# Transposing the second graph layer's weight through two PSUM banks instead of four, one batch earlier on VectorE

## Chip, cores and metric

The kernel runs on one core of a Trainium2 chip. The metric is the device time of one execution in microseconds (us). Engines are named as in the profile: PE is TensorE (PEld its weight loads), DVE VectorE, ACT ScalarE, POOL GpSimd, SP the engine that issues most DMAs.

## What is computed

The input is x (1250 nodes x 512, f32) and a list of 40,000 edges `src`, `dst`, sorted by `dst`. Four layers are added to x one after the other, each on the layer norm of what it gets:

```python
x = x + _L0_gnn_ref(_layernorm(x), edge_index, L0_gnn_Ws, L0_gnn_Wb, L0_gnn_a_w, L0_gnn_a_b)   # 8-head graph attention
x = x + _L0_ffn_ref(_layernorm(x)[None], L0_ffn_Wg, L0_ffn_bg, L0_ffn_We, L0_ffn_be)[0]          # one expert of 16, for all nodes
x = x + _L1_gnn_ref(_layernorm(x), edge_index, L1_gnn_W, L1_gnn_b)                               # h = x @ W.T + b, normed sum over edges, relu
x = x + _L1_ffn_ref(_layernorm(x)[None], L1_ffn_Wr, ..., L1_ffn_b2)[0]                           # one expert of 8 per node
```

The change concerns `L1_gnn_W` (512 x 512), which the third layer multiplies by in transposed form. The transposing is done long before that layer, during the first one.

## The kernel before

Nodes lie in T = 10 tiles of 128, features in K = 4 blocks of 128. The engines run one instruction stream each, in the order written, and meet only at semaphores.

**The counting stage.** The edges are turned into a dense matrix C of counts (source x target). 184 pairs of an edge group and a window of 16 targets are handled in NB = 23 batches of LB = 8 pairs. All four loops below run over the same batches b = 0 to 22, each engine at its own place:

- DVE makes the one-hot matrices of a batch in two halves, `half_onehots(b, 0)` and `half_onehots(b, 1)`, each two instructions of line 916 (one for L_ring, one for R_ring) and each adding 4 to the semaphore `onehots`. The rings hold two batches, so a half waits (line 929) until the pairs of batch b - 2 that used the same half are counted.
- PE runs for each pair `count` (three matmuls, line 1382, waits for `onehots`) and `merge` (one matmul, line 1389, adds what C holds). The order on PE is merge of pair k, count of pair k + 1, then `between(b, k)`. After k = 5 it also loads the addresses of the next batch into registers (line 1457, the helper of line 290).
- ACT copies the counts of each pair back into C (line 531). Pair k of PE's merge waits for the copy of pair k - 1.

**Work that rides along** in the same loops, for b in BEGIN (one tile t = b - 1 for b = 1 to 10): layer norm statistics on DVE (line 815), the normed rows on ACT (517), their transpose on PE (1295), the copy and the rest in f16 (509, 838), then the linear layer of the attention on PE, `lin_a` (1341, 1342) in batch b + 2, and its evacuation on DVE, `evac_a` (858, 860) in batch b + 4, between the two halves. The last tile, t = 9, has its `lin_a` in batch 12 and its `evac_a` in DVE's batch 14, followed there by `scores()` (864 to 867), which gives the thresholds of the attention.

**The second graph layer's weight.** B_GW = 12. For k = 0 to 3:

- PE: `second_weights(k)` in batch 12 + k, after pair 6: four transposes (line 1354) into the bank `gw_bank(k)`, one of the PSUM banks 6, 2, 4, 3. It waits for the last or the last but one `evac_a` (line 1352), since `lin_a` used banks 2 to 5.
- ACT: at the end of batch 12 + k, `gWT[:, 0, k, :]`, the high f16 part (line 600), signals `weight_hi`.
- DVE: at the start of its batch 15 + k, before `half_onehots`, waits for `weight_hi` and takes the low f16 part from the same bank (line 949), signals `weight_lo`.

**The thresholds.** B_CS = 17. PE transposes them after pair 6 of that batch (`thresholds`, line 1362) into banks 3, 4 and 5, after all four `weight_lo`. ACT copies them out at the end of the batch (604), SP writes them to DRAM (338) and reads them back spread over the partitions (343).

After batch 22 ACT loads its Exp table and makes four exponentials (606 to 609), DVE the first head's values (988), and the attention's main stage begins (633, 1025, 1030 and the matmuls of 1486).

Of the kernel before, what the change touches and what calls it, by code (L numbers as in the profile page):

```python
# [16 lines left out]
T = (NODES + P - 1) // P  # L17
NP = T * P
LAST = NODES - (T - 1) * P
K = D // P  # L20
# [35 lines left out]
BEGIN = {1 + t: t for t in range(T)}  # L56
LIN_SLOTS = ((0,), (1, 2), (), (3, 4), (5, 6), (7,), (8, 9), (10, 11))
B_GW = max(BEGIN) + 2
B_CS = B_GW + K + 1
EPS = 1e-5  # L60
FILL_H = 24
SLOPE = 0.2
# [2 lines left out]
def gnn_ffn_kernel(nc, x_d, src_d, dst_d, Ws_d, Wb_d, aw_d, ab_d, Wg_d, bg_d, We_d, be_d, gW_d, gb_d,  # L65
                   Wr_d, br_d, W1_d, b1_d, W2_d, b2_d, out_d):
    ctx = ExitStack()
    with ctx:
# [5 lines left out]
        def sem(name):  # L74
            if name not in sems:
                sems[name] = ctx.enter_context(nc.semaphore(name))
            return sems[name]
# [189 lines left out]
        bank = [ctx.enter_context(nc.psum_tensor(f"bank{i}", [P, 512], F32)) for i in range(8)]  # L267
# [20 lines left out]
        def targets(engine, off):  # L288

            _, at = nc.values_load_multi_w_load_instructions(  # L290
                wk[0:1, bass.ds(off, LB)], engines=[engine], min_val=0, max_val=NP - WN,
                skip_runtime_bounds_check_because="the groups' windows come from targets in 0 to NP, clipped to the last window")
            return at
# [3 lines left out]
            return bank[(0, 1, 7)[(base + k) % 3]] if isinstance(base, int) else bank[k % 2]  # L297

        def gw_bank(k):
            return bank[(6, 2, 4, 3)[k]]  # L300

        def counts_at(at, k):

# [195 lines left out]
        def _(a):  # L499
# [73 lines left out]
            for b in range(NB):  # L573
# [23 lines left out]
                if b - B_GW in range(K):  # L597
                    k = b - B_GW
                    a.wait_ge(sem("gwT_psum"), k + 1)
                    act(gWT[:, 0, k, :], gw_bank(k)[:, :], ACT.Copy, scale=WS).then_inc(sem("weight_hi"), 1)  # L600
                if b == B_CS:
                    for i, n in enumerate((4, 4, 2)):
# [199 lines left out]
        def _(v):  # L802
# [9 lines left out]
            def ln_stats(n, xt, keep=None):  # L812
                i = n % 2
                m = mv[:, i, :] if keep is None else keep
                link(V.bn_stats(st[:, i, :], xt))  # L815
                link(V.bn_aggr(m, st[:, i, :]))
                V.tensor_scalar(ve[:, i:i + 1], m[:, 1:2], EPS, None, ALU.add).then_inc(sem("ln_var"), 1)  # L817
# [11 lines left out]
            def ln_scale(n):  # L829
                i = n % 2  # L830
                v.wait_ge(sem("ln_sd"), n + 1)
                link(V.reciprocal(rs[:, i:i + 1], sd[:, i:i + 1]))
                V.scalar_tensor_tensor(nm[:, i:i + 1], mv[:, i, 0:1], -1.0, rs[:, i:i + 1], ALU.mult, ALU.mult).then_inc(sem("ln_rs"), 1)  # L833

            def xT_low(n, b, xt16):

                v.wait_ge(sem("xT_hi"), n + 1)
                V.tensor_tensor(xt16[:, 1, :, :], b[:, :].rearrange("p (k m) -> p k m", k=K), xt16[:, 0, :, :],
                                ALU.subtract).then_inc(sem("xT_ready"), 1)
# [16 lines left out]
            def evac_a(t):  # L856
                v.wait_ge(sem("linA"), t + 1)
                V.scalar_tensor_tensor(Wx[:, t, :, 0:F], bank[2 + t % 2][:, :].rearrange("p (h f) -> p h f", h=H), 1.0 / WS, Wb_bc,
                                       ALU.mult, ALU.add)
                V.scalar_tensor_tensor(sc[:, t, :], bank[4 + t % 2][:, 0:2 * H], 1.0 / WS, cb, ALU.mult, ALU.add).then_inc(sem("evacA"), 1)  # L860

            def scores():
                v.wait_ge(sem("evacA"), T)
                link(V.tensor_tensor(atb, sc[:, :, 0:H], ab_bc.unsqueeze(1).to_broadcast([P, T, H]), ALU.add))
                V.tensor_scalar(thr, atb, -1.0, None, ALU.mult).then_inc(sem("thr_made"), 1)
                V.tensor_scalar(steep, sc[:, :, H:2 * H], STEEP, None, ALU.mult)
                V.tensor_reduce(asmax, sc[:, :, H:2 * H].rearrange("p t h -> p h t"), AX.X, ALU.max).then_inc(sem("asmax"), 1)
# [16 lines left out]
            def passes():  # L884
                link(V.tensor_scalar(kt[0:1, :], iotaK[0:1, 0:MAXPASS], float(NPAIR), None, ALU.mult))
                link(V.tensor_scalar(kt[0:1, :], kt[0:1, :], bank[4][0:1, NPAIR:NPAIR + 1], None, ALU.is_lt))
                link(V.tensor_reduce(grp[0:1, 6:7], kt[0:1, :], AX.X, ALU.add))
                V.tensor_copy(npass[0:1, :], grp[0:1, 6:7]).then_inc(sem("npass_ready"), 1)
# [36 lines left out]
            def half_onehots(b, half):  # L925
                n = LC // 2
                c = slice(half * n, (half + 1) * n)
                e = slice(b * LC + half * n, b * LC + (half + 1) * n)
                at_least(v, "counted", (b - 2) * LB + (half + 1) * (LB // 2))
                onehot(L_ring[:, b % 2, c, :], iota_lo, loT[:, e, :], n, P)  # L930
                onehot(R_ring[:, b % 2, c, :], iota_q, qT[:, e, :], n, RW).then_inc(sem("onehots"), LB // 2)

            def first_onehots():
                n = LC // 4
                for q in range(4):
                    c = slice(q * n, (q + 1) * n)
                    onehot(L_ring[:, 0, c, :], iota_lo, loT[:, c, :], n, P)
                    onehot(R_ring[:, 0, c, :], iota_q, qT[:, c, :], n, RW).then_inc(sem("onehots"), LB // 4)

            pair_tables(0)  # L940
            for b in range(NB):
                if b == 1:
                    v.wait_ge(sem("ld_x"), 64)
                if b in BEGIN:
                    ln_stats(BEGIN[b], x[:, BEGIN[b], :])
                if b - 3 - B_GW in range(K):
                    k = b - 3 - B_GW
                    v.wait_ge(sem("weight_hi"), 2 + k + 1)
                    V.scalar_tensor_tensor(gWT[:, 1, k, :], gw_bank(k)[:, :], WS, gWT[:, 0, k, :],
                                           ALU.mult, ALU.subtract).then_inc(sem("weight_lo"), 1)  # L950
                if b:
                    half_onehots(b, 0)
                    if b - 4 in BEGIN:
                        evac_a(BEGIN[b - 4])
                        if BEGIN[b - 4] == T - 1:
                            scores()
                    half_onehots(b, 1)
                else:
                    first_onehots()
                    passes()  # L960
                if b == 2:
                    v.wait_ge(sem("weight_hi"), 1)
                    V.scalar_tensor_tensor(W016[:, 1, :, :], W0.rearrange("p k h f -> p k (h f)"), WS, W016[:, 0, :, :],
                                           ALU.mult, ALU.subtract).then_inc(sem("weight_lo"), 1)
                if b == 3:
                    v.wait_ge(sem("weight_hi"), 2)
                    V.scalar_tensor_tensor(Wa[:, 1, :, :].rearrange("p k c -> p (k c)"), bank[5][:, 0:K * 2 * H], WS,
                                           Wa[:, 0, :, :].rearrange("p k c -> p (k c)"), ALU.mult, ALU.subtract).then_inc(sem("weight_lo"), 1)
                if b - 1 in BEGIN:
                    ln_scale(BEGIN[b - 1])  # L970
                if b - 2 in BEGIN:
                    t = BEGIN[b - 2]
                    xT_low(t, bank[6], xTs[:, t % 2, :, :, :])
# [316 lines left out]
        def _(pe):  # L1290
# [55 lines left out]
            def second_weights(k):  # L1346

                if k == 0:
                    pe.wait_ge(sem("xT_ready"), T)
                    pe.wait_ge(sem("ld_gw"), 16)  # L1350
                if k >= 1:
                    pe.wait_ge(sem("evacA"), T if k == K - 1 else T - 1)
                for o in range(K):
                    ins = nc.tensor.transpose(gw_bank(k)[:, o * P:(o + 1) * P], gW[:, o, k * P:(k + 1) * P], ident[:, :])
                ins.then_inc(sem("gwT_psum"), 1)

            def thresholds():
                pe.wait_ge(sem("thr_made"), 1)
                pe.wait_ge(sem("weight_lo"), 2 + K)
                for i, n in enumerate((4, 4, 2)):  # L1360
                    for q in range(n):
                        ins = nc.tensor.transpose(bank[3 + i][0:H, q * P:(q + 1) * P], thr[:, 4 * i + q, :], ident[:, :])
                    ins.then_inc(sem("thrT_psum"), 1)
# [49 lines left out]
            def between(b, k):  # L1413
# [12 lines left out]
                if k == LB - 2:  # L1426
                    if b - B_GW in range(K):
                        second_weights(b - B_GW)
                    if b == B_CS:
                        thresholds()  # L1430
# [281 lines left out]
```

## Time and profile before

| what | us |
|---|---|
| median of the 3 runs | 585.64 |
| lowest and highest of them | 584.92, 589.37 |
| the profiled execution | 585.64 |
| its span in the profile | 583.9 |
| part of it outside the span | 1.74 |
| mean granted clock of PE | 0.96 of full |

The span starts with the first instruction and ends with the last. A row of a timeline gives the start, the duration, the engine, line and operation, and in brackets how long the engine sat idle before it and who released it. DVE and ACT rows overlap their successor by some 0.08 to 0.1 us at their end, so times of a sequence are best taken from start to start. The chain of waits leads back from the last instruction, at each step to what released it.

### The profile page before, as it was taken

The numbers are of one execution on the slowest core, as the hardware profiler recorded it, in microseconds if no ns is written. First come the engines' busy times: TensorE is split into PE (matmuls) and PEld (weight loads), VectorE is DVE, ScalarE is ACT, GpSimd is POOL, SyncE is SP. The second block draws the span as 40 slices with busy tenths as digits, with TensorE's granted clock in tenths as the row PEclk, the third lists the DMA queues.
The fourth block names the chain that finished last, engine by engine and source line by source line (L and its number), as shares of the span: only waits on it lengthen the run. The fifth ranks groups of instructions, "written<-read, shape, count | busy, mean of one in ns | idle before, by whom it ended". The sixth has DMA issues, their size and how long they took to land.

```text
span 583.9 us, 11915 instructions
## 1 busy us (share of the span) xinstructions
PE 502.4 (86%) x4561; PEld 371.5 (64%) x4562; DVE 460.2 (79%) x907; ACT 331.2 (57%) x644; POOL 70.9 (12%) x83
## 2 busy tenths in 40 slices
PE   1869999987579999998999479996999967999995
PEld 1757777775468888887777334453566636767752
DVE  7989999898899999986898556875565645786781
ACT  5365555667879999985674423344222218665740
POOL 3000000000000000000000300213233320222242
PEclk9989999999699999999999689999999977999999
DMA  7960000011011111100000183000011149367111
GB/s 192 358 238 2 1 2 1 3 33 63 0 47 47 47 47 48 46 3 1 1 2 2 50 326 147 1 1 3 0 39 38 55 154 382 111 207 234 58 52 49
DMA packets 25305, 45.12 MB, mean 77 GB/s; under 512 B 6961, under 2 KB 7205, under 8 KB 25248
## 3 DMA queue, kind: packets, MB, share of 16 engines
q1 hardware_dynamic: 23264, 39.16, 19.7%
q0 software_dynamic: 1952, 5.18, 2.4%
q8 instruction: 38, 0.62, 0.5%
q14 instruction: 19, 0.16, 0.1%
q10 hardware_dynamic: 32, 0.01, 0.0%
HBM read 33.23 MB, written 11.95 MB: 77 GB/s over the span
## 4 chain that ended last, share of the span: by engine, by line
PE 47%; DVE 32%; issue 11%; ACT 4%; POOL 3%; DMA 1%; ACTq 1%; POOLq 0%; DVEq 0%
PE bank L1317 8%; PE bank L1654 7%; PE bank L1642 6%; DVE big L916 6%; PE bank L1341 4%; DVE work L1030 4%; PE bank L1382 4%; PE bank L1389 3%; PE bank L1499 2%; PE bank L1486 2%; PE bank L1564 2%; PE bank L1295 2%; DVE rings L1030 2%; POOL row L475 2%; DVE work L988 2%
## 5 line engine op out<-in xcount | busy, mean ns | idle before, releaser
L916 DVE TENSOR_TENSOR big<-mid 128x1536 f16<-128x1536 f16 (+1 forms) x96 | 91.6, 1011 | 0.0
L1486 PE MATMUL bank<-big,work 128*128 128x130 f16 x1080 | 67.8, 224 | 12.0 <-DVE work L1030 11.6
L1382 PE MATMUL bank<-big 128*128 128x160 f16 x552 | 72.2, 248 | 2.6 <-DVE big L916 2.6
L1486 PEld LDWEIGHTS bank<-big,work 128*128 128x128 f16 x1080 | 64.2, 100 | 14.6 <-DVE work L1030 7.5
L1382 PEld LDWEIGHTS bank<-big 128*128 128x128 f16 x552 | 52.0, 111 | 4.8 <-DVE big L916 4.2
L1564 PE MATMUL bank<-mid 128*128 128x512 f16 x200 | 45.9, 379 | 3.3 <-POOL mid L449 3.3
L633 ACT ACTIVATE mid<-aux,small 128x1280 f16<-128x1280 f32 x36 | 47.4, 1350 | 1.5 <-DVE work L1030 1.1
L1499 PE MATMUL bank<-big,mid 128*128 128x260 f16 x400 | 47.2, 275 | 0.1
L531 ACT ACTIVATE big<-bank 128x160 f32 x92 | 28.0, 304 | 27.4 <-PE bank L1389 25.9
L1499 PEld LDWEIGHTS bank<-big,mid 128*128 128x128 f16 x400 | 38.2, 96 | 7.5 <-issue 0.3
L531 ACT ACTIVATE mid<-bank 128x160 f32 x92 | 27.8, 302 | 25.4 <-PE bank L1389 24.2
L815 DVE BATCH_NORM_STATS2 st<-row 128x6 f32<-128x512 f32 x40 | 27.7, 692 | 17.9 <-POOL row L475 17.2
L504 ACT ACTIVATE sd<-ve 128x1 f32<-128x1 f32 x40 | 8.1, 201 | 57.2 <-DVE ve L817 57.2
L1341 PE MATMUL bank<-big,rings 128*128 128x512 f16 x120 | 38.6, 378 | 0.0
L459 POOL DMA_INDIRECT out<-aux x16 | 25.8, 1611 | 81.6 <-DVE aux L1232 79.2
L1389 PE MATMUL bank<-mid,ident 128*128 x92 | 28.1, 305 | 8.2 <-ACT big L531 4.0
L1295 PE MATMUL bank<-ident,rings 128*128 128x128 f32 x120 | 19.4, 285 | 17.8 <-ACT rings L517 15.3
L1486 PE MATMUL bank<-big,rings 128*128 128x130 f16 x520 | 32.0, 220 | 2.9 <-DVE rings L1030 1.9
L1564 PEld LDWEIGHTS bank<-mid 128*128 128x128 f16 x200 | 19.6, 101 | 23.5 <-issue 3.8
L1486 PEld LDWEIGHTS bank<-big,rings 128*128 128x128 f16 x520 | 29.9, 98 | 4.0 <-DVE rings L1030 2.4
L444 POOL TENSOR_TENSOR mid<-mid,ident 128x128 f16<-128x128 f16 x10 | 5.3, 564 | 212.4 <-PE bank L1499 212.4
L517 ACT ACTIVATE rings<-row,nm,rs 128x512 f32<-128x512 f32 x30 | 24.3, 810 | 10.6 <-DVE nm L833 10.6
(293 smaller groups left out, 1090.5 us busy)
## 6 DMA issues: line engine op xcount, KB each, us to landing
big<-in_L_ffn_W SPq DMA_DIRECT2D x10, 1024.0 KB, 9.0
mid<-in_L_ffn_W SPq DMA_DIRECT2D x6, 1024.0 KB, 13.6
xperm_scratch<-work SPq DMA_DIRECT2D x1, 5753.0 KB, 19.2
aux<-thr_scratch SPq DMA_DIRECT2D x8, 640.0 KB, 3.8
aux<-xperm_scratch SPq DMA_DIRECT2D x8, 523.0 KB, 3.7
row<-in_x SPq DMA_DIRECT2D x1, 2304.0 KB
aux<-in_L_gnn_Ws SPq DMA_DIRECT2D x4, 256.0 KB, 4.4
work<-in_L_gnn_W SPq DMA_DIRECT2D x1, 1024.0 KB, 14.4
```

What stands on the lines that cost most here:

```text
L531: ins = act(counts_at(at[k], k), count_bank(base, k)[:, 0:RW].rearrange("p (d s) -> p s d", s=T), ACT.Copy)
L633: act(zmask[i % NZ], thr_bc[:, h % 2, :], ACT.Sigmoid, bias=steep[:, s, h:h + 1], scale=-STEEP).then_inc(sem("z_made"), 1)
L916: return V.tensor_tensor(out.rearrange("p c (v two) -> p c v two", two=2), values.rearrange("p (v two) -> p v two", two=2).unsqueeze(1).to ...
L1030: V.tensor_tensor(weighted[i % NC], zmask[m % NZ], C[:, s, :], ALU.mult).then_inc(sem("cz_made"), 1)
L1317: ins = mm(out, xt16[:, xp, k, :], w16[:, wp, k, :], start=i == 0 and k == 0, stop=i == 2 and k == K - 1)
L1341: mm(bank[2 + t % 2][:, :], xt, W016[:, wp, k, :], start=j == 0, stop=last)
L1382: mm(count_bank(base, k)[:, 0:RW], L_ring[:, slot, k * CH + j, :], R_ring[:, slot, k * CH + j, :], start=j == 0, stop=False)
L1389: ins = mm(count_bank(base, k)[:, 0:RW].rearrange("p (d s) -> p s d", s=T), ident16[:, :], counts_at(at[k], k), start=False, stop=True)
L1486: ins = mm(acc_region(h, t), weighted[i % NC][:, t * P:(t + 1) * P], VP[:, s, part, h, :, :].rearrange("p b f -> p (b f)"), start=False, s ...
L1499: ins = mm(bank[2 * (t % 2) + g2][:, 0:4 * FE].rearrange("p (h f) -> p h f", f=FE), C[:, s, t * P:(t + 1) * P], VP[:, s, part, 4 * g2:4 * ...
L1564: ins = mm(bank[6 + t % 2][:, :], C[:, s, t * P:(t + 1) * P], hp[:, s, part, :], start=s == 0 and part == 0, stop=s == T - 1 and part == 1)
L1654: ins = mm(bank[4 + 2 * (e % 2) + j][0:m, :], hT16[:, e % 2, hp_, k, j * P:j * P + m], W16[e % 2][1][:, wp, k, :], start=False, stop=n == ...
```

## The change

Only two banks, 6 and 2, serve for the four transposed blocks. PE's `second_weights` for k = 2 and 3 waits until DVE has taken the low part of block k - 2 out of the bank. DVE takes the low part of block k at the start of batch 14 + k instead of 15 + k. The thresholds are transposed and copied in batch 16 instead of 17. ACT's copies of the high part stay where they are.

```diff
-B_CS = B_GW + K + 1
+B_CS = B_GW + K
...
         def gw_bank(k):
-            return bank[(6, 2, 4, 3)[k]]
+            return bank[(6, 2)[k % 2]]
...
-                if b - 3 - B_GW in range(K):
-                    k = b - 3 - B_GW
+                if b - 2 - B_GW in range(K):
+                    k = b - 2 - B_GW
                     v.wait_ge(sem("weight_hi"), 2 + k + 1)
                     V.scalar_tensor_tensor(gWT[:, 1, k, :], gw_bank(k)[:, :], WS, gWT[:, 0, k, :],
                                            ALU.mult, ALU.subtract).then_inc(sem("weight_lo"), 1)
...
-                if k >= 1:
-                    pe.wait_ge(sem("evacA"), T if k == K - 1 else T - 1)
+                if k == 1:
+                    pe.wait_ge(sem("evacA"), T - 1)
+                if k >= 2:
+                    pe.wait_ge(sem("weight_lo"), 2 + k - 1)
```

## Rows read from the trace of the kernel before

**Rows 1.** The page: the span, and the costliest group of instructions.

```profile
span 583.9 us, 11915 instructions
...
L916 DVE TENSOR_TENSOR big<-mid 128x1536 f16<-128x1536 f16 (+1 forms) x96 | 91.6, 1011 | 0.0
```

**Rows 2.** Busy time by stretch: stretch, length, engines (instructions), PEclk, DMA share, GB/s.

```profile
80.00:105.50 25.50, 25.18 (x246) 18.82 (x243) 22.93 (x35) 13.39 (x41) 0.00 (x0) 1.00 0.01 2
105.50:123.00 17.50, 15.43 (x161) 13.01 (x158) 17.38 (x24) 11.91 (x40) 0.99 (x1) 1.00 0.01 1
123.00:142.50 19.50, 16.42 (x167) 13.25 (x165) 19.50 (x22) 13.09 (x43) 0.00 (x0) 1.00 0.22 71
```

**Rows 3.** The chain of waits, 105 to 143 us: start, us, what.

```profile
105.55 0.69 DVE mid L858
...
107.14 1.93 DVE big L916 x2
109.08 0.60 DVE mid L949
109.68 3.87 DVE big L916 x4
...
123.09 19.38 DVE big L916 x20
```

**Rows 4.** Timeline of DVE, 96 to 106 us.

```profile
96.53 0.69 DVE L838 TENSOR_TENSOR rings<-bank,rings 128x512 f16<-128x512 f32 x1 [0.76 <-ACT rings L509]
...
100.13 3.95 DVE L916 TENSOR_TENSOR big<-mid 128x1536 f16<-128x1536 f16 x4
105.55 0.69 DVE L858 SCALAR_TENSOR_TENSOR mid<-bank,aux 128x512 f32<-128x512 f32 x1 [1.47 <-PE bank L1342]
```

**Rows 5.** Timeline of ACT, 95 to 134 us.

```profile
95.91 0.59 ACT L509 ACTIVATE rings<-bank 128x512 f16<-128x512 f32 x1
...
105.08 0.59 ACT L600 ACTIVATE mid<-bank 128x512 f16<-128x512 f32 x1
...
109.35 0.59 ACT L600 ACTIVATE mid<-bank 128x512 f16<-128x512 f32 x1
...
117.56 0.59 ACT L600 ACTIVATE mid<-bank 128x512 f16<-128x512 f32 x1
...
129.64 0.30 ACT L531 ACTIVATE mid<-bank 128x160 f32 x1 [0.62 <-PE bank L1389]
...
133.00 0.30 ACT L531 ACTIVATE mid<-bank 128x160 f32 x1 [0.60 <-PE bank L1389]
```

**Rows 6.** Timeline of PE, 104 to 143 us.

```profile
104.07 0.63 PE L1354 MATMUL bank<-ident,work 128*128 128x128 f32 x4
...
110.64 0.41 PE L1382 MATMUL bank<-big 128*128 128x160 f16 x3
...
114.73 0.41 PE L1382 MATMUL bank<-big 128*128 128x160 f16 x3
...
124.14 1.25 PE L1362 MATMUL bank<-ident,small 128*8 128x128 f32 x10
...
142.52 0.38 PE L1382 MATMUL bank<-big 128*128 128x160 f16 x3 [0.37 <-DVE big L916]
```

**Rows 7.** Busy time by stretch, two pairs of shorter stretches.

```profile
28.00:32.00 4.00, 2.02 (x20) 1.41 (x18) 3.51 (x4) 2.23 (x4) 0.00 (x0) 1.00 1.06 372
32.00:36.00 4.00, 2.85 (x16) 2.42 (x16) 3.50 (x7) 2.05 (x8) 0.00 (x0) 0.57 1.05 374
...
110.60:116.00 5.40, 4.73 (x50) 3.92 (x47) 5.40 (x6) 3.86 (x13) 0.00 (x0) 1.00 0.02 5
...
126.00:130.00 4.00, 2.71 (x30) 2.20 (x29) 4.00 (x5) 2.98 (x11) 0.00 (x0) 1.00 0.10 14
```

**Rows 8.** The chain of waits, 483 to 499 us: two experts' first linear layer.

```profile
483.91 7.10 PE bank L1642 x48
...
493.94 4.44 PE bank L1642 x48
```

**Rows 9.** Timeline of PE at a lower granted clock, 33 to 35 us.

```profile
33.35 0.47 PE L1389 MATMUL bank<-big,ident 128*128 x1
...
34.01 0.47 PE L1389 MATMUL bank<-mid,ident 128*128 x1
```

## Prediction

> **What bounds the kernel now.** I read the page first, then the busy time by stretch for the counting stage, then the chain of waits and the three timelines around 100 to 125 us, where the change acts. The one-hot instructions of line 916 are the costliest group of the kernel, 91.6 us in 96 instructions, with no idle time before them [rows 1]. The stage has two parts. From 80 to 105.5 us PE is full (25.18 of 25.50 us) while DVE is busy for 22.93; after that DVE is full (17.38 of 17.50, then 19.50 of 19.50) and PE is not [rows 2]. The chain says the same and gives the point of handover: it runs on PE until the last `lin_a`, passes to DVE's line 858 at 105.55, and then stays on DVE, through every one-hot half and all four instructions of line 949, until 142.5 [rows 3]. PE's next count waits for DVE there (142.52, idle 0.37) [rows 6]. So from 105.55 on, whatever DVE does or waits for in this stage moves the end of the stage.
>
> Before that point DVE has slack, and it is all in one place: it finishes four instructions of line 916 that began at 100.13 and then sits idle 1.47 us for `lin_a` of the last tile [rows 4]. By the order of the code these four are `half_onehots(13, 1)` and `half_onehots(14, 0)`. At 3.87 us for four [rows 3] a half takes 1.935.
>
> **DVE's low parts, one batch earlier: the term that counts.** Block 0 now stands at the start of batch 14, between `half_onehots(13, 1)` and `half_onehots(14, 0)`. DVE reaches it at 100.13 + 1.94 = 102.07. It waits for `weight_hi`, and that instruction does not move: PE's transposes of block 0 start at 104.07 in batch 12 [rows 6], ACT's copy runs from 105.08 to 105.67 [rows 5]. ACT's line 509 ended at 95.91 + 0.59 = 96.50 and the DVE instruction that waited for it started at 96.53 [rows 4, 5], so block 0 starts at 105.70. DVE idles 3.6 us where it idled 1.5. Queued behind the wait is `half_onehots(14, 0)`, which before was made in this time; then `evac_a(9)`, whose own wait (over at 105.55) is now covered. From there:
>
> - block 0 of line 949: 0.60, from 105.70 to 106.30;
> - `half_onehots(14, 0)`: 1.935, to 108.24;
> - `evac_a(9)` and `scores()`: before from 105.55 to the 916 pair at 107.14, which the DVE timeline puts some 0.08 earlier; I take 1.51, to 109.75;
> - `half_onehots(14, 1)`: 1.935, to 111.68;
> - block 1: 0.60, two halves 3.87, block 2, two halves, block 3, two halves: 13.41, to 125.09, the start of batch 18.
>
> Before, batch 18 started on DVE at 123.09 - 0.08 = 123.01. The loss is 2.08 us. The shorter way to it: all four line 949 instructions are on DVE's path in both kernels (four times 0.60 either way), the handover comes 0.15 later (105.70 for 105.55), and one half, 1.935, has left the shadow of the wait and stands behind it. 0.15 + 1.935 = 2.08. Below this I see only 0.15 less, if ACT's copy came earlier; above, the later waits, next.
>
> **Blocks 1 to 3 on DVE.** Before, each waited for a copy long done (block 0: wanted at 109.08, there at 105.67). Now the margins are small. PE's count of pair 4 of batch 14 needs `half_onehots(14, 1)`; it ran at 110.64 [rows 6] and can now start at about 111.81 (the DVE slot plus 0.13 for end and signal, as at 142.39 to 142.52). So PE stalls 1.2 us and follows DVE half by half from batch 14 on. From that count in batch 15 (114.73) to the end of ACT's copy in that batch (117.56 + 0.59) it is 3.42 us [rows 5, 6]. Block 1 needs ACT's copy at 109.35 + 0.59 = 109.94, which the stall does not touch; DVE asks at 111.68. Block 2: 111.81 + 3.42 = 115.2, DVE asks at 116.15. Block 3: PE counts at 116.28, the copy is there at 119.7, DVE asks at 120.62. No wait, with 1.7, 0.9 and 0.9 us to spare. I take 0; the upper bound is in the rivals.
>
> **PE's new waits.** `second_weights(2)`, in batch 14, waits for block 0's low part, done at 106.3; PE gets there at about 112.47 + 1.2 = 113.6. Block 3 waits for block 1's, done at 112.3, some 5 us ahead. The `evacA` wait of block 1 was met at about 100.2 in both. Cost 0, gain 0: the four banks bought nothing by themselves; if PE did wait, the counts of the batch behind it would be late, and through them DVE in its ring two batches on.
>
> **Thresholds in batch 16.** PE's ten transposes take about 1.1 us from 124.14 [rows 6] and ACT's three copies about 1.2. They move into the batch right after the last block. Their wait (block 3's low part, about 121.2) is over when PE comes, about 122.6. PE then lags the halves by up to 1.1 + 1.2 us. An undisturbed batch on PE takes 3.36 (ACT's copies 129.64 to 133.00 [rows 5]) against 3.87 on DVE, so it recovers 0.5 per batch, by batch 20 or 21 of 22; DVE's ring wait reaches two batches back and isn't hit. Cost 0, where without this spare the last lag would add up to 2.3. The DRAM round trip starts 1 to 2 us earlier; nothing waits for it, since what follows the stage is the Exp load and the exponentials. Gain 0.
>
> **PE's granted clock.** In 110.6 to 116 us PE is busy 4.73 of 5.40 us at a granted clock of 1.00; a stall of 1.2 us makes that about 3.6. In 126 to 130 it was busy 2.71 of 4.00 and the clock stayed at 1.00, while after 28 to 32, busy 2.02 of 4.00, it fell to a mean of 0.57 [rows 7], that is, largely the 1.2 GHz level. The nearest row is the one at 1.00, so I take no change. The Trainium skill, page "TensorE: Matmul & The Clock Gate", section "A second HAM failure mode: psum-queue depth-cycling", speaks against a change of this kind: a kernel that cycles through PSUM banks idles TensorE in small steps until the clock swings between its levels. By that rule batches 14 to 22 could run at the lower level; the price is the last rival's. By the row, the sum stays.
>
> **The sum.** All behind the stage follows it in a row, so the span is 583.9 + 2.1 = 586.0 and the time 586.0 + 1.74 = 587.7. The profiled execution is itself the median of the three runs (585.64), so nothing is converted. That is 0.36% more.
>
> **Rivals.**
>
> *Not slower: the low clock of the last stage falls elsewhere.* The first expert's first layer takes 7.10 us, the next 4.44, for the same 48 matmuls [rows 8]. The first runs after PE's waits for tokens, at a lower clock. If the shift of all that is ahead changed where the clock comes back, up to 2.66 us would go: 587.72 - 2.66 = 585.1. It decides from the point where 2.08 of the 2.66 are saved. For it: runs of the same kernel differ by 0.7 us and once by 4. Against it: what precedes that stage moves along with it unchanged. Chance 0.08.
>
> *DVE's stall hidden.* If something other than DVE set the end of the stage, the time would stay at 585.6. Twenty 916s in 19.38 us without a gap [rows 3] speak against it. That the low parts fill DVE's old idle time (so that up to 0.6 is won, 585.0) needs the copy before 104.08, and it comes at 105.67. Chance 0.03 together.
>
> *Lockstep.* If the margins of 0.9 us are gone (PE's lag larger than I think), blocks 1 to 3 each wait for ACT's copy. With 1 us each that is 3 more: 590.7. For it: DVE and PE then wait for each other in turn. Against it: the 3.42 us is measured, against the 4.47 us of a DVE batch with its block. Chance 0.06.
>
> *The clock falls in the stage.* At the lower level pairs follow each other by 34.01 - 33.35 = 0.66 us [rows 9], 5.28 for eight, more than DVE's 3.87. From the count at 111.81 eight batches would end at 154.1 instead of 144.6: 9.5 more, 597.2. A stretch of 4 us would cost some 1.5 of PE's lag and be recovered. Chance 0.03.
>
> **How the numbers follow.** The forecast has 0.80. Its own range is 587.72 - 0.15 to about 588.7 from the terms, and the runs of before scatter from -0.7 to +3.7 around their median, rarely far. I take 585.5 to 590.2 as the range: it leaves out part of the not slower cases and nearly all of the last two. A measurement of this kernel can tell about 1% from no change. Slower by over 1% (over 591.5) is the last rival and an edge of lockstep, 0.04; faster by over 1% has no mechanism, 0.01; within 1%, 0.95.
>
> **What would show it.** Right: DVE idle about 3.6 us before the first line 949, released by ACT's line 600, and none before line 858; the four 949s at about 105.7, 111.7, 116.1 and 120.6 without idle before the last three; PE idle about 1.2 us before a count near 111.8, released by DVE's 916; the last wait of PE at 144.6 for 142.5; the span 586.0. Wrong in a step: idle before the second to fourth 949 (lockstep), idle before lines 1354 or 1362 (bank waits), a clock under 1.00 between 110 and 142 us. The prediction is wrong if the first 949 starts well before 105.7, or if the stage ends 2 us later and the span does not.

## The result, and the profile after

| | us |
|---|---|
| changed kernel, median of 20 runs (lowest, highest) | 590.58 (588.0, 593.85) |
| kernel before, median of 20 runs beside it | 589.1 (584.01, 596.81) |
| ratio, 95% interval | 1.006 (1.0032 to 1.0088) |
| profiled execution of the changed kernel, its span | 591.3, 589.5 |

The changed kernel is slower, as forecast in direction; the forecast of 1.0036 lies inside the interval of the ratio, near its lower end. The ratios here and below take only runs within 1.5% of the fastest run of their kernel, and that leaves out four of these 20 runs of the kernel before (593.28 to 596.81) and none of the changed kernel's, which raises this one. By all 20 runs of each the means are 589.03 and 590.96, 0.33% apart, and the medians 0.25%. The time itself lies just outside the range given (585.5 to 590.2), because the kernel before had a median 3.5 us higher here than in the three runs that the prediction started from.

The spans of the two profiled executions differ by 5.6 us, and most of that is not the change. First the place of the change. The timeline of DVE in the changed kernel, 98 to 108 us, answers to [rows 4]:

```profile
98.21 0.69 DVE L858 SCALAR_TENSOR_TENSOR mid<-bank,aux 128x512 f32<-128x512 f32 x1 [0.28 <-PE bank L1342]
98.82 0.17 DVE L860 SCALAR_TENSOR_TENSOR small<-bank,small 128x16 f32<-128x16 f32 x1
98.90 2.02 DVE L916 TENSOR_TENSOR big<-mid 128x1536 f16<-128x1536 f16 x2
104.47 0.69 DVE L949 SCALAR_TENSOR_TENSOR mid<-bank,mid 128x512 f16<-128x512 f32 x1 [3.56 <-ACT mid L600]
105.08 2.02 DVE L916 TENSOR_TENSOR big<-mid 128x1536 f16<-128x1536 f16 x2
107.02 0.68 DVE L858 SCALAR_TENSOR_TENSOR mid<-bank,aux 128x512 f32<-128x512 f32 x1
```

The row of line 916 shows two instructions where there were four; the other two come after line 949, which waited 3.56 us for ACT's copy. Line 858, which waited 1.47 us, waits for nothing. The chain of waits from there on answers to [rows 3]:

```profile
104.47 0.69 DVE mid L949
105.16 1.93 DVE big L916 x2
107.10 0.60 DVE mid L858
...
108.60 1.93 DVE big L916 x2
110.53 0.60 DVE mid L949
111.13 3.87 DVE big L916 x4
115.00 0.60 DVE mid L949
115.60 3.87 DVE big L916 x4
119.48 0.60 DVE mid L949
120.08 23.26 DVE big L916 x24
```

The last three of line 949 follow the ones before without a gap. Four rows of PE's timeline answer to [rows 6]:

```profile
110.59 0.38 PE L1384 MATMUL bank<-big 128*128 128x160 f16 x3 [0.97 <-DVE big L916]
...
112.18 0.60 PE L1356 MATMUL bank<-ident,work 128*128 128x128 f32 x4
...
121.13 1.25 PE L1364 MATMUL bank<-ident,small 128*8 128x128 f32 x10
...
143.38 0.38 PE L1384 MATMUL bank<-big 128*128 128x160 f16 x3 [0.37 <-DVE big L916]
```

Lines of PE's block are two higher than before. PE waits 0.97 us for the late half, then follows DVE; no idle time stands before any of the transposes (1356) or the thresholds (1364).

The stage ends only 0.86 us later by the clock of the trace (143.38 for 142.52), since everything ahead of the change came 1.23 us earlier in this execution (line 858 of tile 8 at 98.21 for 99.44). So from here on a stretch is measured whose start the change can't touch: from line 858 of tile 8, which DVE runs in its batch 13, to ACT's Exp table load (line 606). This stretch is called the stage below. It is 144.44 - 99.44 = 45.00 us before, and 145.31 - 98.21 = 47.10 after: 2.10 us more, 2.08 forecast.

**The other 3.5 us of the two spans.** I split both profiles at the same instructions:

| from, to | before | after |
|---|---|---|
| start to line 858 of tile 8 | 99.44 | 98.21 |
| to the Exp table load (the stage) | 45.00 | 47.10 |
| to the router of the second layer (1083) | 185.93 | 185.92 |
| to its first result (1106) | 14.54 | 14.03 |
| to the first addition of the third layer (475) | 66.6 | 68.2 |
| to the last of these additions | 51.6 | 51.6 |
| to the first expert's first matmul (1642) | 20.8 | 23.2 |
| to the end | 100.0 | 101.2 |

In front of the first addition PE's first 28 aggregation matmuls took 7.89 us instead of 6.20, at a granted clock of 0.73 in 408 to 413 us where it had been 1.00; in both kernels PE had sat idle for 3.29 us before them. The row of PE's timeline in the kernel before, and in the changed one:

```profile
406.11 6.20 PE L1564 MATMUL bank<-mid 128*128 128x512 f16 x28 [3.29 <-POOL mid L449]
```

```profile
406.47 7.89 PE L1566 MATMUL bank<-mid 128*128 128x512 f16 x28 [3.29 <-POOL mid L449]
```

In the last stretch the first layers of the first two experts took 7.10 and 4.44 us before, and in the chain of waits of the changed kernel:

```profile
488.38 6.50 PE bank L1644 x48
...
498.25 6.10 PE bank L1644 x48
```

Together they are 1.06 us longer, at a granted clock of 0.70 in 489 to 495 us and 0.76 in 500 to 506. Ahead of the first expert it was POOL's last scatter of tokens (line 467). POOL and DVE in the kernel before:

```profile
472.76 0.99 POOL L467 DMA_INDIRECT xperm_scratch<-row,small  x1 [0.30 <-issue]
...
472.94 2.27 DVE L1131 SCALAR_TENSOR_TENSOR mid<-big,mid 128x2048 f16<-128x2048 f32 x1
```

and in the changed one:

```profile
474.75 2.27 DVE L1131 SCALAR_TENSOR_TENSOR mid<-big,mid 128x2048 f16<-128x2048 f32 x1
474.81 3.08 POOL L467 DMA_INDIRECT xperm_scratch<-row,small  x1 [0.31 <-issue]
```

Where POOL starts 0.18 us ahead of DVE's long instruction it takes 0.99, where it starts 0.06 behind it takes 3.08 and ends 0.87 after DVE's end (477.02). The Trainium skill, page "SBUF — State Buffer", section "SBUF: two separate sides", says that these two engines share a pair of ports which the one that starts first keeps for its whole instruction, while the other blocks; for a VectorE instruction with two SBUF inputs, as here, it says so only against a GpSimd instruction that reads SBUF. The two profiles agree for POOL. For DVE they don't show it: its instruction took 2.27 us also where POOL had started first, and 2.28 or 2.29 in the four runs below in which it stands well behind the last scatter. Whether these effects belong to the change is what the later experiments ask.

### The profile page after: what moved, and what is told of

Its sections match the earlier page's. It is cut to its first block, busy times and chain, and to the rows that moved or that the text cites. A ratio compares the mean times of both kernels' runs of the same rounds, so it can differ in the third digit from the quotient of the medians.

```text
span 589.5 us, 11915 instructions
## 1 busy us (share of the span) xinstructions
PE 505.1 (86%) x4561; PEld 372.5 (63%) x4562; DVE 459.9 (78%) x907; ACT 331.9 (56%) x644; POOL 73.2 (12%) x83
## 3 DMA queue, kind: packets, MB, share of 16 engines
q1 hardware_dynamic: 23264, 39.16, 19.4%
## 4 chain that ended last, share of the span: by engine, by line
PE 47%; DVE 32%; issue 11%; ACT 4%; POOL 3%; DMA 2%; ACTq 0%; POOLq 0%; DVEq 0%
PE bank L1317 8%; PE bank L1656 7%; DVE big L916 7%; PE bank L1644 6%; PE bank L1341 4%; DVE work L1030 4%; PE bank L1384 3%; PE bank L1391 3%; PE bank L1566 3%; PE bank L1501 2%; PE bank L1488 2%; PE bank L1295 2%; DVE rings L1030 2%; POOL row L475 2%; DVE work L988 2%
## 5 line engine op out<-in xcount | busy, mean ns | idle before, releaser
L1488 PE MATMUL bank<-big,work 128*128 128x130 f16 x1080 | 68.2, 225 | 11.1 <-DVE work L1030 11.1
L1566 PE MATMUL bank<-mid 128*128 128x512 f16 x200 | 47.6, 389 | 3.3 <-POOL mid L449 3.3
L1295 PE MATMUL bank<-ident,rings 128*128 128x128 f32 x120 | 19.4, 285 | 17.7 <-ACT rings L517 15.2
```

The source lines that it names most:

```text
L1488: ins = mm(acc_region(h, t), weighted[i % NC][:, t * P:(t + 1) * P], VP[:, s, part, h, :, :].rearrange("p b f -> p (b f)"), start=False, s ...
L1566: ins = mm(bank[6 + t % 2][:, :], C[:, s, t * P:(t + 1) * P], hp[:, s, part, :], start=s == 0 and part == 0, stop=s == T - 1 and part == 1)
```

## The experiments

Each kernel had 12 runs beside the kernel before on the same chip. The ratios have intervals of about plus or minus 0.4 to 0.5%, wider than the effect; the stage of the profiled execution is the sharp measure. It rests on one execution each, but kernels in which it should be the same agree within 0.02 us.

| kernel | stage, us | against before | ratio (95%) |
|---|---|---|---|
| before | 45.00 | | |
| the change | 47.10 | +2.10 | 1.006 (1.0032 to 1.0088) |
| e1_two_banks_only | 45.00 | 0 | 1.0019 (0.9971 to 1.0066) |
| e2_low_earlier_only | 47.09 | +2.09 | 1.0048 (1.0005 to 1.0091) |
| e3_low_between_halves | 45.00 | 0 | 1.0003 (0.9949 to 1.0058) |
| e4_one_half_twice | 47.18 | +2.18 | 1.0028 (0.9986 to 1.0069) |
| e5_low_after_stage | 43.68 | -1.32 | 0.9971 (0.9933 to 1.0008) |
| e6_transposes_after_lin | 44.53 | -0.47 | 1.001 (0.9964 to 1.0055) |
| e8_more_fill | 45.01 | 0 | 0.999 (0.995 to 1.003) |
| e9_more_fill_after | 47.10 | +2.10 | 1.0034 (0.9993 to 1.0075) |
| e10_split_later | 45.02 | 0 | 1.0022 (0.9984 to 1.0059) |
| e12_split_later_after | 47.10 | +2.10 | 1.0036 (0.9999 to 1.0073) |
| e11_split_later_low_after_stage | 43.66 | -1.34 | 0.9969 (0.9934 to 1.0004) |
| e13_e11_again | 43.66 | -1.34 | 0.9972 (0.9931 to 1.0014) |

### The banks alone

To the changed kernel:

```diff
-B_CS = B_GW + K
+B_CS = B_GW + K + 1
...
-                if b - 2 - B_GW in range(K):
-                    k = b - 2 - B_GW
+                if b - 3 - B_GW in range(K):
+                    k = b - 3 - B_GW
```

> Of the change only the two banks and PE's waits for them are kept; DVE's low parts are back at the start of batch 15 + k, the thresholds in batch 17. Theory (one half of one-hots has moved behind a wait): the first low part again finds its copy done, DVE idles 1.5 us before line 858 and nothing before line 949, PE's new waits cost nothing; ratio to before 1.000, the start of the last one-hot run as in before. Rival (sharing two banks costs): PE idles before the transposes of blocks 2 and 3, and the ratio is nearer to the full change's 1.006.

DVE's timeline of this run:

```profile
107.75 0.69 DVE L858 SCALAR_TENSOR_TENSOR mid<-bank,aux 128x512 f32<-128x512 f32 x1 [1.47 <-PE bank L1342]
```

The old 1.47 us of idle is back, the stage is 45.00. Two banks cost nothing, and the rival falls by the stage, not by the ratio, whose interval holds 1.006. The profile of this run also has the later stretches of the changed kernel, without its delay: 68.2 us to the first addition, 23.2 to the first expert and 101.2 to the end. So has that of e8, which changes neither banks nor batches (68.2, 23.2 and 101.2). What made the two spans differ beyond the stage thus comes without the delay too.

### DVE's low parts alone

To the kernel before:

```diff
-                if b - 3 - B_GW in range(K):
-                    k = b - 3 - B_GW
+                if b - 2 - B_GW in range(K):
+                    k = b - 2 - B_GW
```

> The kernel before with one thing of the change: DVE's low parts one batch earlier. Four banks, thresholds in batch 17. Theory: all of the change's loss, 3.6 us of idle before the first line 949, the counting stage 2.1 us longer from the copy of block 0 on; ratio 1.0035 if nothing else follows, up to the 1.006 measured for the whole change if what follows in the clock of PE belongs to the shift. Rival (banks or thresholds carry part of it): clearly less than the full change.

```profile
104.81 0.69 DVE L949 SCALAR_TENSOR_TENSOR mid<-bank,mid 128x512 f16<-128x512 f32 x1 [3.56 <-ACT mid L600]
```

This row of DVE's timeline has the same 3.56 us as the full change, and the stage is 47.09. One edit carries the whole loss.

### The same batch, behind the first half

To the changed kernel; the five lines of the low part move:

```diff
                if b:
                    half_onehots(b, 0)
                    if b - 4 in BEGIN:
                        evac_a(BEGIN[b - 4])
                        if BEGIN[b - 4] == T - 1:
                            scores()
+                    if b - 2 - B_GW in range(K):
+                        k = b - 2 - B_GW
...
                    half_onehots(b, 1)
```

> The whole change, but each low part stands between the two halves of its batch (in batch 14 behind evac_a and scores) instead of ahead of both. Theory: half_onehots(14, 0) is made in the shadow of the last lin_a again, the first line 949 finds its copy there since 1.4 us, and the 2.1 us are gone: ratio 1.000 to before. Rival (the batch in which the low part stands is what costs, or the banks): the ratio stays near 1.006.

```profile
105.69 0.69 DVE L858 SCALAR_TENSOR_TENSOR mid<-bank,aux 128x512 f32<-128x512 f32 x1 [1.47 <-PE bank L1342]
...
107.19 0.68 DVE L955 SCALAR_TENSOR_TENSOR mid<-bank,mid 128x512 f16<-128x512 f32 x1
```

In DVE's timeline the low part (here line 955) has no idle time before it, and the stage is 45.00 again, with two banks, the same batches and the earlier thresholds. It is not the batch that cost 2.1 us but the one half of one-hots behind the wait. In this order PE does wait for the last low part, ahead of the thresholds, as its timeline shows:

```profile
121.43 1.25 PE L1364 MATMUL bank<-ident,small 128*8 128x128 f32 x10 [0.47 <-DVE mid L955]
```

The 0.47 us are recovered before the stage ends.

### A plain delay of the same size

To the kernel before:

```diff
                if b:
+                    if b == 18:
+                        n = LC // 2
+                        at_least(v, "counted", (b - 2) * LB + LB // 2)
+                        link(onehot(L_ring[:, b % 2, 0:n, :], iota_lo, loT[:, b * LC:b * LC + n, :], n, P))
+                        link(onehot(R_ring[:, b % 2, 0:n, :], iota_q, qT[:, b * LC:b * LC + n, :], n, RW))
                    half_onehots(b, 0)
```

> The kernel before; DVE makes the first half of batch 18 twice (same values, two instructions of line 916 more, each waited for). This is a plain delay of about 2.0 us in the part where DVE sets the pace, with no change to banks or waits. Theory: the stage ends 2.0 us later, and the time grows as in the full change, ratio 1.0034 by the delay alone. Rival 1: a delay of this size is amplified later by PE's granted clock; the ratio is 1.006 as in the full change. Rival 2: the delay is absorbed; ratio 1.000.

The chain of waits has the added pair, and the run of 19.4 us follows as before:

```profile
121.92 0.88 DVE big L916
...
122.82 1.17 DVE big L916
...
124.01 19.47 DVE big L916 x20
```

The added pair takes 2.09 us from its start to the next row (121.92 to 124.01), and the stage is 2.18 us longer: in this part DVE's time is the stage's time. The ratio of 12 runs can't choose between 1.0034 and 1.006; the pooled runs below can say more.

### More off DVE's path

To the kernel before:

```diff
+GW_AT = {12: 0, 13: 1, 18: 2, 19: 3}
...
-                if b - 3 - B_GW in range(K):
-                    k = b - 3 - B_GW
-                    v.wait_ge(sem("weight_hi"), 2 + k + 1)
-                    V.scalar_tensor_tensor(gWT[:, 1, k, :], gw_bank(k)[:, :], WS, gWT[:, 0, k, :],
-                                           ALU.mult, ALU.subtract).then_inc(sem("weight_lo"), 1)
...
             exponents()
+            for k in range(K):
+                v.wait_ge(sem("weight_hi"), 2 + k + 1)
+                V.scalar_tensor_tensor(gWT[:, 1, k, :], gw_bank(k)[:, :], WS, gWT[:, 0, k, :],
+                                       ALU.mult, ALU.subtract).then_inc(sem("weight_lo"), 1)
...
-                    if b - B_GW in range(K):
-                        second_weights(b - B_GW)
+                    if b in GW_AT:
+                        second_weights(GW_AT[b])
```

(ACT's copies go by GW_AT too; PE waits for the thresholds' copies before block 2, and for the four low parts before the attention's matmuls.)

> From the kernel before: all four low parts leave the counting stage and stand behind DVE's last one-hots and exponents(), where DVE idled 3.05 us for ACT's Exp table and exponentials. Blocks 0 and 1 are transposed in batches 12 and 13 (banks 6 and 2), blocks 2 and 3 in batches 18 and 19 (banks 4 and 3, after the thresholds' copies). Theory (all that DVE does in that part is on the path): four times 0.60 = 2.4 us off the stage, nothing added behind it (2.4 of work in 3.05 of idle), so from evac_a of tile 8 to the Exp table load 42.6 us instead of 45.0, ratio 0.996. Rival (PE sets the pace as soon as DVE is 2.4 us shorter, or the four wait longer behind the stage than the idle time): 44 us or more, ratio 0.999 or above.

It gained 1.32 us, not 2.4. DVE's timeline behind the stage, and the chain:

```profile
142.19 0.25 DVE L873 TENSOR_TENSOR small<-small 128x80 f32<-128x80 f32 x1
```

```profile
141.50 0.31 PE bank L1390
...
145.01 0.30 ACT big L532
...
145.33 1.28 ACT L607
```

DVE is through with the one-hots at 142.19 and the Exp load comes 3.14 us later; in the kernel before the same two points were 142.39 and 144.44, 2.05 us apart. 1.09 of the 2.4 us went to PE, on which the chain now runs through the stage. So the rival was partly right, though its 44 us weren't reached: DVE had only 1.3 us to give before PE sets the pace.

### Block 0's transposes behind the last linear part

To the kernel before:

```diff
-                if k == LB - 2:
-                    if b - B_GW in range(K):
+                if k == LB - 1 and b == B_GW:
+                    second_weights(0)
+                if k == LB - 2:
+                    if b - 1 - B_GW in range(K - 1):
                         second_weights(b - B_GW)
```

> From the kernel before: PE's transposes of block 0 come after the last lin_a of batch 12 instead of ahead of its last two parts. Theory (the path runs over PE up to lin_a and over DVE from there): lin_a, evac_a and all behind it 0.49 us earlier, DVE's idle before line 858 1.0 instead of 1.5, the low part still finds its copy done; 44.5 us from evac_a of tile 8 to the Exp table load instead of 45.0; ratio 0.999. Rival (the copy, now later, holds up the counts and then DVE's ring): no gain or a loss.

The row of line 858 for the last tile:

```profile
107.34 0.69 DVE L858 SCALAR_TENSOR_TENSOR mid<-bank,aux 128x512 f32<-128x512 f32 x1 [1.00 <-PE bank L1342]
```

It waited 1.00 us instead of 1.47, and the stage is 0.47 us shorter (0.49 expected). The ratio says nothing about so little. One of the 12 runs took 2816.88 us; nothing on record explains it.

### Filling matmuls against the lower clock

To the kernel before (e8) and to the changed one (e9):

```diff
-FILL_H = 24
+FILL_H = 44
```

> From the kernel before: 44 instead of 24 of PE's filling matmuls (results unused) before the first expert, to cover PE's idle time for the tokens (477.4 to 481.5 us). Theory on the scatter (runs of one kernel differ by up to 10 us because the granted clock falls and returns at different places): the first expert's first layer takes about 4.5 instead of 7.1 us, the median falls by 2 to 3 us and the spread narrows. Rival (the low clock there is not due to the idle time): no change in either; the fills may even delay the tokens' transposes where they run at the lower clock.

> The changed kernel with the same 44 filling matmuls as e8_more_fill. Theory: against e8_more_fill the changed kernel is 2.1 us longer in the counting stage, and if the scatter is less here, the two medians show that difference more sharply (0.36%). Rival (the change costs more than its 2.1 us by a fixed effect later on): the difference of the medians stays at 3.5 us or more.

The chain in e8_more_fill, around the first expert:

```profile
489.53 6.48 PE bank L1642 x48
```

6.48 us, not 4.5: PE still waited 2.0 us for the tokens and 1.3 us for their low part, and in 490 to 500 us its granted clock was 0.81. The idea of a cover did not work here, and the times scatter as before (585.63 to 592.59). Both stages are as they should be. The median of e9 lies 2.1 us above that of e8, the mean 2.5, plus or minus 1.9: that fits the stage, but does not exclude e9's rival of 3.5.

### DVE's long instruction out of the scatter's way

To the kernel before (e10) and to the changed one (e12):

```diff
             V.tensor_copy(nspill[0:1, :], cum[0:1, E1 - 1:E1]).then_inc(sem("te_ready"), 1)
-            split_w(1, 0)
...
             names(1)
+            split_w(1, 0)
             split_w(1, 1)
```

> Cause sought for the part of the difference that does not lie in the counting stage. In the profile of before POOL's last scatter (line 467) started 0.18 us ahead of DVE's long instruction of line 1131 (2.27 us) and took 0.99 us; in the changed kernel's it started 0.06 us behind it and took 3.08 us, and the tokens landed 2.1 us later. This is the kernel before with that instruction (the low part of the second expert's first weight, on DVE) moved behind the naming of the first tokens, next to the other split. Theory A (an order race between POOL and DVE, decided by tenths of a us): the last scatter takes 1.0 us in the profile, the runs at the upper end go, and the median falls by 1 to 2 us (ratio 0.998). Theory B (the scatter's length has another cause): 3.1 us as often as before, ratio 1.000. If the split now delays the first experts, ratio above 1.001.

> The changed kernel with the same move. Theory A: its last scatter takes 1.0 us, it gains more than the kernel before does from the same move if its runs stood more often on the wrong side of the race, and against e10_split_later it is 2.1 us longer (0.36%), which is the counting stage alone. Theory B: the difference between the two stays at 3 us or more, with the scatter at 3.1 us or not.

POOL's last scatter in e12_split_later_after, the changed kernel with this move:

```profile
474.83 0.99 POOL L467 DMA_INDIRECT xperm_scratch<-row,small  x1 [0.30 <-issue]
```

0.99 us, also in e10, e11 and e13. Of the ten other profiled executions, all with the split in its old place, eight have 3.08 to 3.12, and DVE starts 0.03 to 0.06 us ahead in each; two (before and e5) have 0.99, and there POOL starts 0.18 us ahead. That the order of the two engines decides the scatter's length is shown. That it explains the kernel's time is not. None of e10's 12 runs is above 590.6, where 9 of the 29 runs of the kernel before beside it are, but its ratio to before is 1.0022 with 1 inside, and its mean (588.9) is not clear of the 589.2 of all runs of before. In e12, with the short scatter too, three of 12 runs are above 591, up to 593.45. Its mean is 1.3 us above that of e10, plus or minus 1.6, and its median 0.6 below: that holds the stage's 2.1 us and can't show it.

### The version that beats both

> e5_low_after_stage (all low parts behind the counting stage, 43.7 us from evac_a of tile 8 to the Exp table load instead of 45.0) together with the later split of e10_split_later. If the two gains add: 1.3 us and what e10 gives, ratio 0.995. If the scatter isn't what differs, ratio 0.997 as e5 alone.

> e11_split_later_low_after_stage once more, for a narrower interval: twelve runs of kernels that scatter over 8 us can't tell 0.3% from nothing. Theory (1.3 us off the counting stage for certain, the scatter's 2.1 us in a part of the runs): ratio 0.994 to 0.998, no run above 591. Rival (e11's lower times were the luck of the runs): ratio within 0.999 to 1.001 and runs up to 593.

e11 joins the edits of e5 and e10; e13 is the same kernel again. Medians of 586.05 and 586.1 beside 588.23 and 589.31 of before, each ratio with 1 just inside. Both together are 24 runs with a mean of 586.9, the highest at 590.51. Against the 46 runs of before on the same chip that is 1.8 us less, plus or minus 1.2, and against all 136 runs of before 2.3, plus or minus 0.9. 1.34 of it is the stage; that the later split gives anything on top is not shown, since e11's ratio is the 0.997 expected of e5 alone. The expectation's "no run above 591" held, its ratio of 0.994 to 0.998 too.

### All runs pooled

The kernel before ran 136 times in five groups of runs. Its mean is 589.2, from 584.0 to 596.8. The three kernels that carry the delay of 2.1 us and nothing else that matters (the change, e2, e4; 44 runs) have a mean of 591.4. Difference 2.2 us, plus or minus 0.8 (1.96 standard errors from the scatter of the runs; the runs were made on several occasions). That is 0.37% and agrees with the delay alone; an amplification to 3.5 us or more lies outside. With e9 and e12 added, which carry the delay too (68 runs), the difference is 2.0, plus or minus 0.7.

One thing stays open. 49 of the 136 runs of before are below 588 us, and none of these 44 is, nor of the 68. The lower edge has thus moved by 4 us, the mean by 2.2. The scatter race alone isn't the reason: e12 has its short scatter and no run below 588 either (588.88 is its lowest). The mean granted clock alone isn't it either: at 0.960 ten runs of before took 584.2 to 586.0 us, and the change's eight took 588.0 to 588.8. One thing fits in size. The stretch from the first result to the first addition takes 66.5 or 68.2 us, and it took 68.2 in all five profiles with the delay, 66.5 in three of the nine without it; 1.7 us there and 2.1 of delay make 3.8. Five profiles are too few to show it.

## Why the prediction was right, and where it was wrong

- *DVE's low parts, the term that counts.* Right to 0.02 us: idle 3.56 (3.6 forecast), stage +2.10 (2.08). The short reckoning, one half behind the wait plus the later handover, is confirmed from three sides: e2 has it with this edit alone, e3 loses it by moving the instruction behind the half, e4 makes the same delay out of a half done twice.
- *Blocks 1 to 3.* No wait, as forecast. Copies of blocks 2 and 3 were there at 113.74 and 118.25, asked for at 114.92 and 119.39: 1.2 and 1.1 us to spare, 0.9 forecast. Lockstep did not come. PE's stall before its count was 0.97 us, where 1.2 was forecast.
- *PE's new waits.* Zero (e1).
- *Thresholds.* Zero in the change. With the low part later (e3) PE waited 0.47 us for them and recovered it, as the spare of 0.5 us per batch allows.
- *Granted clock in the stage.* In 110.6 to 116 and 126 to 130 us of the changed kernel it was 1.00, as in [rows 7], and 1.00 through the whole stage in every profile. The swing between the two levels that the Trainium skill, page "TensorE: Matmul & The Clock Gate", section "A second HAM failure mode: psum-queue depth-cycling", tells of did not come here, with PE idle for 0.97 us once and for 0.2 to 0.9 us again and again.
- *The stall hidden.* Refuted: the stage is 2.10 us longer, and e4's plain delay shows in it as well.
- *The sum: wrong in its base.* The step that failed is "The profiled execution is itself the median of the three runs (585.64), so nothing is converted", with "the runs of before scatter from -0.7 to +3.7 around their median, rarely far". 585.64 was a low draw, and a range drawn from three runs was too narrow: 34 of 136 runs of the same kernel are at or below it, the median of the groups lies between 588.2 and 590.8. With 589.1 as the base, the same 2.08 us gives 591.2, beside 590.58 measured. "All behind the stage follows it in a row" failed too: in the profiled execution the stretches behind the stage were 4.8 us longer in sum and the one ahead of it 1.2 shorter, so the span was 589.5 and not 586.0. e1 and e8 have the same later stretches without the delay, so this is scatter that the sum had at nothing. What decides it from run to run stays open.
- *The rival of the last stage's clock* argued that "what precedes that stage moves along with it unchanged". It doesn't: line 858 of tile 8, long before the change acts, started between 98.0 and 101.7 us in the fourteen profiles, and the stretch to the first addition took 66.5 to 66.6 us in three of them and 68.2 or 68.3 in eleven. The rival's gain of 2.66 us did not come: in the profile the first of the two layers took 6.50 us instead of 7.10, but the second 6.10 instead of 4.44, and no run of the changed kernel lies under 588. The sort of effect it named, a lower clock at another place, is one part of the scatter that the profiles show.

## What to carry to other kernels

When an instruction with a wait is moved ahead in an in-order stream, look at what used to be done in the shadow of the next wait: that work now stands behind the new one, and its whole length is lost if the engine sets the pace. Placing the moved instruction behind that work (e3) costs nothing. And a forecast of a time, unlike one of a difference, is only as good as the number of runs its base rests on: a stretch between two instructions that the change can't shift measured 2.1 us to 0.1, where 12 runs of the whole kernel could not.

## What the runs showed of the hardware

- POOL's indirect DMA (line 467) took 0.99 us when it started 0.18 us ahead of a DVE instruction with two SBUF inputs (two profiles) and 3.08 to 3.12 when it started 0.03 to 0.06 us behind (eight); with the DVE instruction elsewhere it took 0.99 in four profiles of four. The DVE instruction took 2.27 us in all ten.
- Executions of one kernel on one chip differ by up to 11.7 us with nothing changed (584.49 to 596.16 in the 29 runs of before beside e10); of the change's 32 runs with a clock on record the eight with a mean granted clock of 0.96 took 588.0 to 588.8 us, those at 0.950 or below 589.8 or more, up to 596.8.
- The attention's main stage repeats almost exactly: 185.88 to 185.96 us from the Exp load to the router in all fourteen profiles.
